# Softmax denominators from one summed tile: GpSimd adds the two key halves, TensorE's ones multiply the sum

## The reference

```
q = rms_norm(layernorm(x) @ w_q.T + b_q, g_q)          # 16 heads of 32
k_img = rms_norm(ctx_img @ w_k_img.T + b_k_img, g_k_img)
v_img = ctx_img @ w_v_img.T + b_v_img
s = einsum('bqhd,bkhd->bhqk', q, k) * SCALE
p = softmax(s)                                          # over the 256 keys
x = x + einsum('bhqk,bkhd->bqhd', p, v) @ w_o.T + b_o
...
x = x + ffn(layernorm(x))      # top 2 of 8 experts, clipped gated units
```

## Time and profile before

| what | value |
|---|---|
| times of 3 runs | 863.65, 863.79, 868.08 us |
| median | 863.79 us |
| span of the profiled execution | 869.3 us |
| mean granted TensorE clock in it | 0.955 |
| PE busy | 783.9 us, 90% |
| DVE busy | 625.5 us, 72% |
| ACT busy | 431.3 us, 50% |
| GpSimd busy | 376.0 us, 43% |
| attention stage, about | 45 to 440 us of the span |

### The profile page before, as it was taken

The page is one execution under the profiler, slowest core; times in us unless marked ns, Lnnn a source line. Parts: engine busy times, 40 slices in busy tenths (PEclk is TensorE's granted clock), DMA queues, the critical chain, the costliest instruction groups (busy, mean ns, idle before and its releaser), DMA issues.

```text
span 869.3 us, 16360 instructions
## 1 busy us (share of the span) xinstructions
PE 783.9 (90%) x6501; PEld 639.6 (74%) x6501; DVE 625.5 (72%) x1249; ACT 431.3 (50%) x648; POOL 376.0 (43%) x373
## 2 busy tenths in 40 slices
PE   3989999999999899976789967899999999999995
PEld 3767776777777677754558956889797888979783
DVE  5666676656666565674765877787969797997883
ACT  4434443444345234423434644557658475766752
POOL 3213125252442524235064336275664838475523
PEclk9899999999999999998788989899999999999998
DMA  7999398878969581216255557678795868878663
GB/s 288 280 320 304 120 299 256 267 232 266 302 209 301 196 234 58 92 55 200 102 194 202 195 187 199 172 220 298 206 298 191 250 207 258 257 217 300 178 179 73
DMA packets 60778, 188.25 MB, mean 217 GB/s; under 512 B 5671, under 2 KB 6055, under 8 KB 51102
## 3 DMA queue, kind: packets, MB, share of 16 engines
q0 software_dynamic: 23584, 109.35, 39.9%
q1 hardware_dynamic: 37118, 77.86, 29.9%
HBM read 104.18 MB, written 84.84 MB: 217 GB/s over the span
## 4 chain that ended last, share of the span: by engine, by line
PE 34%; issue 19%; POOL 15%; DMA 14%; DVE 11%; ACT 7%; another core or an unknown queue 1%; POOLq 0%; DVEq 0%; ACTq 0%
DMA raw<-in_wga,wx 6%; PE bank L602 5%; PE bank L668 4%; PE bank L603 4%; PE bank L604 4%; POOL xs L1525 4%; PE bank L576 4%; POOL out L1547 4%; DVE el L1163 3%; DMA hf<-hr,si 3%; ACT eh L1385 3%; PE quad L649 3%; PE quad L629 3%; POOL raw L1535 2%; PE bank L706 2%
## 5 line engine op out<-in xcount | busy, mean ns | idle before, releaser
L1163 DVE TENSOR_TENSOR el<-raw,eh 128x2048 fp32r<-128x2048 f32 x72 | 164.5, 2287 | 42.0 <-ACT eh L1385 40.0
L1385 ACT ACTIVATE eh<-raw 128x2048 fp32r<-128x2048 f32 x72 | 137.4, 1912 | 81.7 <-DMA raw<-in_wga,wx 34.4
L763 PE MATMUL quad<-xh,eh 128*128 128x256 f32 x480 | 139.7, 291 | 0.0
L765 PE MATMUL quad<-xh,el 128*128 128x256 f32 x480 | 136.8, 285 | 0.0
L764 PE MATMUL quad<-xl,eh 128*128 128x256 f32 x480 | 136.8, 285 | 0.0
L966 DVE TENSOR_REDUCE mx<-quad 128x8 f32<-128x2048 f32 x32 | 73.3, 2292 | 51.6 <-PE quad L629 51.0
L1351 ACT ACTIVATE nm<-bank 128x256 fp32r<-128x256 f32 x32 | 12.3, 384 | 172.1 <-PE bank L576 148.1
L1547 POOL DMA_INDIRECT out<-ys,ti x39 | 73.5, 1884 | 52.3 <-ACT ys L1435 33.4
L763 PEld LDWEIGHTS quad<-xh,eh 128*128 128x128 f32 x480 | 93.3, 194 | 0.2
L764 PEld LDWEIGHTS quad<-xl,eh 128*128 128x128 f32 x480 | 93.2, 194 | 0.0
L765 PEld LDWEIGHTS quad<-xh,el 128*128 128x128 f32 x480 | 92.9, 194 | 0.0
(11 more groups left out here) (258 smaller groups left out, 1981.3 us busy)
## 6 DMA issues: line engine op xcount, KB each, us to landing
hs<-wh SPq DMA_DIRECT2D x16, 2084.0 KB, 16.9
hf<-wh SPq DMA_DIRECT2D x10, 2084.0 KB
xt<-in_x SPq DMA_DIRECT2D x8, 512.0 KB, 7.4
cr<-in_ctxT SPq DMA_DIRECT2D x8, 512.0 KB
xb<-in_x SPq DMA_DIRECT2D x8, 512.0 KB
out<-xb SPq DMA_DIRECT2D x16, 256.0 KB
pt<-in_w SPq DMA_DIRECT2D x3, 1024.0 KB, 6.6
pt<-in_w SPq DMA_DIRECT2D x4, 256.0 KB, 6.0
```

What stands on the lines that cost most here:

```text
L763: e.matmul(o, lh, xh[p][:, c, :], start=c == 0, stop=False)
L765: done = e.matmul(o, ll, xh[p][:, c, :], start=False, stop=c == C - 1)
L1163: e.tensor_tensor(wl[p][part][:], raw[part][:, 0:GW], wh[p][part][:].bitcast(F32), ALU.subtract).then_inc(S_(f"e_lo{part}"), 1)
L1385: e.activation(wh[p][part][:], raw[part][:, 0:GW], ACT.Copy).then_inc(S_(f"e_hi{part}"), 1)
```

## The change

For each group GpSimd now adds the two key halves of `pt` into a new tile `psum` (128 x 4 x 256, one buffer) in one instruction. The ones multiply that sum once for each head: four matmuls with `onef` instead of eight. The eight with `vt` come first, then PE waits for the sum. `G.sum0` to `G.sum3` are new in `AT`, 30 other numbers of `AT` and one of `END` are not those of before. The rest of the tables is only wrapped differently.

```diff
 AT = {
-    "hk1": 152, "hq1": 179, "peak0": 187, "peak1": 252, "peak2": 285, "peak3": 336, "m0": 202, "m1": 257, "m2": 318,
...
+    "G.sum0": 242, "G.sum1": 279, "G.sum2": 326, "G.sum3": 357,
...
+        psum = sb(ctx, "psum", [128, 4, S])
...
-                for half_ in range(2):
-                    for t in range(2):
-                        for j in range(4):
-                            c0 = t * D + g * 128 + 32 * j
-                            lhs = onef[:] if half_ else vt[b % 2][:, c0:c0 + 32]
-                            done = e.matmul(bank[7][32 * j:32 * j + 32, half_ * 256:half_ * 256 + 256], lhs,
-                                            pt[v % 2][:, j, t * 256:(t + 1) * 256], start=t == 0, stop=t == 1)
+                for t in range(2):
+                    for j in range(4):
+                        c0 = t * D + g * 128 + 32 * j
+                        e.matmul(bank[7][32 * j:32 * j + 32, 0:256], vt[b % 2][:, c0:c0 + 32],
+                                 pt[v % 2][:, j, t * 256:(t + 1) * 256], start=t == 0, stop=t == 1)
+                P.wait_ge(S_("key_sum"), v + 1)
+                for j in range(4):
+                    done = e.matmul(bank[7][32 * j:32 * j + 32, 256:512], onef[:], psum[:, j, :], start=True, stop=True)
                 done.then_inc(S_("value"), 1)
...
+            def key_sum(b, g):
+                v = 4 * b + g
+                P.wait_ge(S_("prob"), v + 1)
+                P.wait_ge(S_("value"), v)
+                e.tensor_tensor(psum[:], pt[v % 2][:, :, 0:256], pt[v % 2][:, :, 256:512], ALU.add).then_inc(S_("key_sum"), 1)
+
...
+                    for b in at(s, f"G.sum{g}"):
+                        key_sum(b, g)
```

More of the change, by code:

```diff
@@ L103 @@
         "A.us0": 74, "A.us1": 77, "A.us2": 84, "A.us3": 90, "A.ah0": 80, "A.ah1": 85, "A.ah2": 92, "A.ah3": 95,
[1 row of a table removed]
-        "G.add": 116,
[2 rows of a table added]
     },
@@ L201 @@
     "x0": -6, "x1": 50, "k0": -12, "q0": 71, "k1": 117, "q1": 128, "v0": 147, "v1": 180, "hk0": 67, "hq0": 125,
[15 rows of a table removed]
[16 rows of a table added]
 }
 END = {
-    "G.ol3": 385, "r0": 458, "r1": 499, "A.r0": 445, "A.r1": 517, "V.row0": 446, "V.res0": 443, "V.res1": 458,
-    "G.root2_0": 406, "G.root2_1": 473, "V.row1": 489, "router": 499, "V.choose": 524, "A.gap": 527, "V.weigh": 527,
-    "rank": 542, "V.place": 556, "S.out0": 430, "S.out1": 477, "G.slots0": 548, "G.first0": 427, "G.slots1": 589,
-    "G.first1": 488,
[4 rows of a table added]
 }
 ONCE = {
-    "A.w0": -20, "A.w1": 51, "A.w2": 84, "A.w3": 119, "V.w0": -39, "V.rows": 22, "V.first": 84, "V.w1": 64, "V.w2": 94,
-    "V.gates": 353, "V.more": 221, "V.w3": 182, "fold": 170, "experts": 383,
+    "A.w0": -20, "A.w1": 51, "A.w2": 84, "A.w3": 119, "V.w0": -39, "V.rows": 22, "V.first": 84, "V.w1": 64,
+    "V.w2": 94, "V.gates": 353, "V.more": 221, "V.w3": 182, "fold": 170, "experts": 383,
 }
```

## The result

The change made the kernel slower: 874.12 us (median of 20 runs) against 869.04 us for the kernel before in the same runs, a ratio of 1.0064 (95% interval 1.0041 to 1.0087), which is 5.6 us; the two medians lie 5.1 apart. Timed again later it was 875.59 against 869.10, 1.0068 (1.0036 to 1.0100). The forecast of 866.7 us, no change that can be told, and its range up to 873.5 were both missed. The three runs that the forecast started from (863.79) lay low: twenty gave 869.04. The profiled execution took 874.40 us with a span of 872.6.

A forecast was written before the change was run, and what follows sets the result against it. PE was taken to bound attention; gains of 12.8, 3.3 and 2.0 us against losses of 11.3, 6.4, 1.7 and 1.6 made +2.9 us, or 866.7 us on the median of 863.79. The range was 851.5 to 873.5 us.

The forecast's parts named there:

- the bound (PE): In attention PE is the bound, busy 97.53 of 100 us from 200 to 300 us.
- A full group saves: Four ones matmuls instead of eight save 0.44 us a group; over 32 groups, after corrections, 12.8 us gained.
- Group 0's ones of batches 2 to 6: Group 0's sum is queued behind the scatters on GpSimd, so PE waits about 1 us: 5.0 us lost.
- `nm`: Maxima turned ahead of `hn`, so its transposes fill PE's 0.47 us wait in 7 batches: 3.3 us gained.
- `hr`: PE's waits for the normalised rows shrink as `hf` scatters may start sooner against PE: 2.0 us gained.
- The rival in which DVE isn't held: Sums disturb nothing on DVE that matters; 11.3, 1.7 and 1.6 fall away: 852.1 us, chance 0.22.
- the sum of group 3 and `peak0`: The sum holds DVE in `weigh`, `ql` is late and PE waits in `peak0`, batches 0 to 5: 11.3 us lost.
- The gains put down to the order: Waits for `nm` and `hr` that the new order removes: 3.3 and 2.0 us gained.
- The clock: New 2.8 us waits in batches 1 and 3 cause one clock fall in two: 1.7 us lost.
- the last batch: In batch 7 DVE's split `el` and `pr` meet sums: 1.6 us lost, between 0 and 4.9.
- The rival by the clock: Waits beside the router lower PE's clock in batches 0, 1, 3 and the last: 871.8 us, chance 0.26.
- The rule on the ports: DVE and GpSimd share ports locked for a whole instruction, so `weigh` is held in full; without it 11.3 us better.

The follow-up runs named there:

- e4: The change without the sum of group 3, which multiplies eight ones matmuls again: 860.8 us, ratio 0.9918 to the kernel before.
- e11: The changed kernel unedited, one run for a second trace: 876.9 us, where the kernel before took 859.6 in the same set.
- e13: The changed kernel unedited, timed again in rounds: 875.6 us, ratio 1.0068 to the kernel before.
- e14: The change with no sums in batch 7, all four groups summed in batches 0 to 6: 873.2 us, ratio 1.0039 to the kernel before.
- e1: The change's new tables without sums on GpSimd, eight ones matmuls a group as before: 864.3 us, ratio 0.9955 to the kernel before.
- e12: The kernel before, unedited, one run for a second trace: 862.6 us, where its median in the same set was 859.6.
- e5: The change with the sum of group 3 split into four instructions of 256 columns: 864.8 us, ratio 0.9935 to the kernel before.
- e16: The change with sums only in groups 1 and 2 of batches 0 to 6, `val3` ahead of the next `peak0`: 856.5 us, ratio 0.9826 to the kernel before.
- e15: The change with sums only in groups 0 to 2 of batches 0 to 6: 858.2 us, ratio 0.9852 to the kernel before.
- e2: The change's sums and four ones matmuls a group, in the old tables of the kernel before: 886.3 us, ratio 1.0214 to the kernel before.
- e6: The change without the sum of group 3, and group 0's sum moved ahead of the last two `hf` scatters: 877.7 us, ratio 1.0111 to the kernel before.
- e9: The change with sums in groups 1 and 2 alone, eight ones matmuls in the others: 862.0 us, ratio 1.0033 to the kernel before.

## Why the prediction was wrong, by its steps

**Right, and confirmed in place:** the bound (PE), the mechanism and its place. The sum is 2.38 us (2.4 said). A full group saves 0.43 us (0.44 said). Group 2's sum is hidden and group 1's costs 0.2 (its `vt` half takes 1.07 to 1.12 instead of 0.89). Group 0's ones of batches 2 to 6 come 0.61, 0.62, 1.05, 1.02 and 1.35 later, 4.65 in all (5.0 said), and 0.43 to 1.17 of each is wait. `nm` gave 3.4 (3.3 said) and `hr` 3.3 (2.0 said). The rival in which DVE isn't held is out: with the sum of group 3 `tmp` takes 2.48 us, without it (e4) 0.36.

**The level.** Of the 7.4 us between forecast and median, 5.3 are the median of three runs that stood for the kernel before. My last line gave a range in absolute time on a base known from three runs, and did not widen it for that. On the median of twenty runs the same sum gives 871.9, 2.2 below the measured time, and that remainder hangs on the terms that follow.

**The step that was mis-sized: the sum of group 3 and `peak0`**, 11.3 said and 15.9 measured (16.3 and 16.1 in e11 and e13): 8.9 said and 11.4 measured in batches 1 to 5, 2.4 and 4.6 in batch 0. Two parts of it failed.

First, "in three of them (2, 4, 5) the clock falls behind the router anyway ... there PE comes 1.7 later and waits 1.1". I took a clock fall of one trace as belonging to those batches. In the change's trace only batch 4 had it ahead of the wait (0.90 us); the others paid 2.56 to 2.64 in full, and in batches 1 and 2 a fall came behind the wait instead. Busy time by stretch, behind the wait of batch 2, and ahead of that of batch 4:

```profile
188.00:192.00 4.00, 4.00 (x29) 2.35 (x29) 3.41 (x5) 0.00 (x0) 3.50 (x4) 0.57 1.05 286
280.00:284.00 4.00, 4.00 (x42) 3.54 (x42) 3.41 (x16) 2.48 (x4) 2.71 (x4) 0.59 1.06 309
```

e11 has such a short wait in batch 2 (1.18), e13 in batch 3 (0.91), e14 in 1, 3 and 5. Where the fall comes changes from run to run; of two prices, 1.1 and 2.6, the longer is the commoner.

Second, batch 0, 2.4 said and "at most 4.4", measured 4.56. There the sum does not meet `weigh` but the setup of `br`. DVE before, and in the changed kernel:

```profile
83.46 0.74 DVE L937 SCALAR_TENSOR_TENSOR br<-br,cmt,h2t 16x512 fp32r<-16x512 f32 x1
```

```profile
82.27 2.82 DVE L940 SCALAR_TENSOR_TENSOR br<-br,cmt,h2t 16x512 fp32r<-16x512 f32 x1
85.12 0.69 DVE L960 TENSOR_TENSOR ql<-bank,qh 128x512 fp32r<-128x512 f32 x1
```

e1 puts 3.5 of it on the order alone, where I had 2.0, so the sum adds 1.1.

**The gains put down to the order** (3.3 and 2.0) were read from a trace 2.1 us above its own median: 871.1, which is its span of 869.3 and the 1.8 by which the time of the other profiled runs lies above their spans, against 869.0. The `hr` part depends on how scatters land: e12 has none of it. So in a usual run less is gained. With the terms as measured (-12.0 for 28 groups, -3.4, -3.3, +15.7, +4.65, +1.4 for seven groups 1, and -1.5 in batch 7, where ACT's stall was 1.7 shorter) the two first traces should differ by +1.6 at the last exponential. They differ by -0.1; 1.1 of that is that the first exponential already came at 48.17 instead of 49.30, and 0.6 stays unexplained. The profiled span is 3.3 longer, and that lies behind attention, in falls of the clock that e13 (18.3 us lost there, as before) does not have.

That these terms add up to less than I forecast (+1.6 against +2.9), though the largest was 4.4 too small (15.7 net of the 0.15 that was waited before), is luck. The clock (1.7 said) came to nothing, the last batch (1.6 said) came out 1.5 shorter with most of it ACT's stall, and `hr` gave 1.3 more than said. With the 2.1 by which the trace of before lay high, +1.6 makes +3.7, which the interval of the measured ratio (3.6 to 7.6 us) just holds. This is a sum that fits and not a proof: what a median run of either kernel loses to the clock behind attention is not on record.

**The rival by the clock** did not come true: from 45 to 380 us both first traces lose the same to the clock, 6.8 us in four falls of 1.7 each. There are falls behind the waits of batches 0, 1 and 2, as that rival said, but of the four that the kernel before had there, in batches 2, 4 and 5 and behind the wait in 5, only that of batch 4 is left.

**The rule on the ports.** By the Trainium skill, "SBUF — State Buffer", section "SBUF: two separate sides", the lock lasts for a whole instruction; the traces agree: `tmp` ended 0.03 us after the sum, and four pieces hold less than one. I had taken the whole 2.4 us as the price of the work, when it was that of one instruction, and for e5 I expected the pieces to hold as long.

## What to carry to other kernels

A GpSimd instruction over SBUF can keep a DVE step waiting until its own end. Held here were steps with two SBUF inputs (`dd`, `oht`, `hr`, `br`) and the cast `ixf` and the TENSOR_SCALAR `tmp` from SBUF to SBUF; not held were steps that read PSUM, and BATCH_NORM_STATS2 (0.69 us) and RECIPROCAL (0.20 us) on one SBUF input. So look at what DVE does in the very microseconds it is to run in, and cut it into pieces, or do without it where a small step of DVE ends a wait of TensorE. Here sums in two or three groups of four and none in the last batch (e16, e15) gave a gain that four in four turned into a loss.

Before an instruction is put into an in-order queue, list what stands ahead of it that waits (the `ol` in e2) and what stands behind it that something waits for (the scatters in e6); the first cost TensorE 2.3 us a batch and the second about 3.

A forecast of a few parts in a thousand needs the base from more than three runs, and a clock fall seen in one trace is to be priced as one that may stand elsewhere.

## What the hardware showed that I had not expected

- Four adds of 256 columns take 2.80 us in all, one of 1024 takes 2.38. The longer way was 1.3% better for the kernel.
- Most traces have a stall of ACT of 2.2 to 4.9 us in front of one exponential of batch 7, whose releaser the profile puts down as remote; the four traces of one set (e9 to e12) have none. Its cause is open.
- In that set the kernel before was 9 to 11 us faster than in the others, with no wait for scatters. The change was not (876.9, one run). Why scatters landed sooner is open.
